# Attention scores in a one-core ViT block: keys spread by DMA replaced by 32-row tiles of TensorE

## The reference, cut to what matters

```python
q1 = heads(x @ Q1_w.T);  k1 = heads(x @ K1_w.T + K1_b)      # heads: 8 of width 16
q2 = heads(x @ Q2_w.T);  k2 = heads(x @ K2_w.T + K2_b)
a1 = softmax(einsum('bhqd,bhkd->bhqk', q1, k1) / scale)
a2 = softmax(einsum('bhqd,bhkd->bhqk', q2, k2) / scale)
attn = a1 - lam * a2
o = einsum('bhqk,bhkd->bhqd', attn, v)
```

## Time and profile before

| | |
|---|---|
| median of 3 runs | 238.61 us |
| lowest and highest run | 237.48 and 258.14 us |
| profiled execution, its own time | 233.28 us |
| its span, first to last instruction | 231.5 us |
| PE busy | 181.9 us (79%) |
| DVE busy | 150.4 us (65%) |
| ACT busy | 102.6 us (44%) |
| POOL busy | 47.6 us (21%) |
| TensorE clock granted, mean | 0.884 |

### The profile page before, as it was taken

The page is one execution under the profiler, slowest core; times in us unless marked ns, Lnnn a source line. Parts: engine busy times, 40 slices in busy tenths (PEclk is TensorE's granted clock), DMA queues, the critical chain, the costliest instruction groups (busy, mean ns, idle before and its releaser), DMA issues.

```text
span 231.5 us, 8246 instructions
## 1 busy us (share of the span) xinstructions
PE 181.9 (79%) x3649; PEld 142.6 (62%) x3649; DVE 150.4 (65%) x335; ACT 102.6 (44%) x185; POOL 47.6 (21%) x64
## 2 busy tenths in 40 slices
PE   0799989999186595787899999999999999992000
PEld 0799975558144364675478888788887787871000
DVE  1333596567459999789965776666555454468960
ACT  2000047557213322413353667776775343325882
POOL 0000007302508668300000000000007000007660
PEclk9999999999859855558999999999999999998555
DMA  6999994253446400000000222131200000000012
GB/s 228 396 391 387 401 146 98 78 129 92 117 107 141 92 6 3 4 3 0 4 0 3 52 58 78 30 96 34 80 5 3 3 6 3 3 3 4 28 45 71
DMA packets 11108, 19.83 MB, mean 86 GB/s; under 512 B 2030, under 2 KB 6830, under 8 KB 10432
## 3 DMA queue, kind: packets, MB, share of 16 engines
q1 hardware_dynamic: 11072, 19.30, 28.5%
HBM read 15.20 MB, written 0.82 MB: 69 GB/s over the span
## 4 chain that ended last, share of the span: by engine, by line
PE 47%; DVE 31%; SPq 6%; issue 5%; ACT 4%; DMA 3%; POOL 2%; ACTq 0%; POOLq 0%
PE PS L1086 14%; PE PS L898 10%; DVE arena L302 7%; PE PS L1108 7%; PE PS L1098 4%; DVE t L649 3%; SPq L363 3%; DVE sm L703 2%; DVE mx L691 2%; ACT t L610 2%; SPq L350 2%; DVE st L851 2%; PE PS L1056 2%; PE PS L935 2%; DMA hid<-conv_filter 2%
## 5 line engine op out<-in xcount | busy, mean ns | idle before, releaser
L302 DVE COPY arena<-PS 128x1024 f32<-128x1024 f32 x32 | 39.0, 1224 | 32.4 <-PE PS L1086 32.4
L301 ACT ACTIVATE arena<-PS 128x1024 f32<-128x1024 f32 x32 | 32.7, 1025 | 22.4 <-PE PS L1086 22.3
L1086 PE MATMUL PS<-gates,wrow 18*128 18x128 f32 x1024 | 37.2, 282 | 1.7 <-DVE arena L302 0.7
L1086 PEld LDWEIGHTS PS<-gates,wrow 18*128 18x128 f32 x1024 | 31.4, 186 | 7.9 <-DVE arena L302 5.0
L898 PE MATMUL PS<-hid,arena 128*128 128x128 f32 (+1 forms) x208 | 26.7, 288 | 7.3 <-DVE hid L628 7.3
L898 PEld LDWEIGHTS PS<-hid,arena 128*128 128x128 f32 (+1 forms) x208 | 25.2, 198 | 8.7 <-issue 8.3
L957 PE MATMUL PS<-hid,arena 128*32 128x200 f32 x256 | 16.7, 421 | 10.0 <-DMA hid<-arena 10.0
L628 DVE TENSOR_REDUCE hid<-hid 128x256 f32<-128x1280 f32 x4 | 9.5, 2369 | 16.8 <-DMA hid<-conv_filter 16.8
L459 ACT ACTIVATE sd<-mv,epsc 128x2 f32<-128x2 f32 (+1 forms) x15 | 4.3, 292 | 35.7 <-DVE mv L639 35.7
L957 PEld LDWEIGHTS PS<-hid,arena 128*32 128x32 f32 x256 | 9.2, 132 | 16.3 <-DMA hid<-arena 11.8
L1108 PE MATMUL PS<-arena,t 128*32 128x128 f32 x512 | 17.3, 276 | 0.0
(11 more groups left out here) (106 smaller groups left out, 294.1 us busy)
## 6 DMA issues: line engine op xcount, KB each, us to landing
arena<-windows SPq DMA_DIRECT2D x24, 256.0 KB, 7.9
wrow<-ffn_weights SPq DMA_DIRECT2D x32, 128.0 KB
hid<-arena SPq DMA_DIRECT2D x32, 100.0 KB, 2.2
hid<-conv_filter SPq DMA_DIRECT2D x4, 640.0 KB, 7.3
cst<-consts SPq DMA_DIRECT2D x1, 1098.0 KB, 16.6
wrow<-ffn_weights SPq DMA_DIRECT2D x64, 8.0 KB
out<-t SPq DMA_DIRECT2D x16, 50.0 KB
arena<-windows SPq DMA_DIRECT2D x4, 64.0 KB, 8.1
```

Source lines behind the costliest of these rows:

```text
L301: return eng.activation(dst, PS[:, b:b + 2, :], ACT.Copy)
L302: return eng.tensor_copy(dst, PS[:, b:b + 2, :])
L1086: mm = pe.matmul(PS[:, merge_bank(n) + r, :].rearrange("p (b k j) -> p k b j", k=4, j=NJ)[:, k], wrow[32 * r:32 * r + KR, w], gates[32 * r ...
```

## The change

The spread keys go, and with them the zeroed buffer, its semaphores and the 32 DMAs. `scores(u)` takes its keys straight from `kX`. It now goes by 32-channel blocks r = 0 to 3: for each block, each b and each of the 8 images one matmul, whose stationary operand is 32 channels by 32 query columns (partitions 32r to 32r+31) and whose moving operand is 32 channels by 50 columns (25 keys with the odd head zeroed, 25 with the even one zeroed). That is 64 matmuls of 50 columns a step, where there were 16 of 200. Blocks 0 and 2 write one PSUM bank, blocks 1 and 3 the other; between block 1 and block 2, PE waits until its own last matmul of block 1 is done (`half_scored`). Each step waits for all four projections of its images instead of the spread keys. The scores of a step lie in another order of heads, so the layouts of `E`, `prob`, `probT` and of the weights `lamw` change with them; the number and size of these operations stays as it was.

```diff
-        prob = take(2 * 4 * H * 32).rearrange("p (n g h k) -> p n g h k", n=2, g=4, h=H)
-        kE = hid[:, 0:2 * 2 * H * UI * NS].rearrange("p (s b h i k) -> p s b h i k", s=2, b=2, h=H, i=UI)
-        kEd = hid[:, 0:2 * 2 * H * UI * NS].rearrange("p (s b r c) -> p s b r c", s=2, b=2, r=4)
+        prob = take(2 * 4 * H * 32).rearrange("p (n r x k) -> p n r x k", n=2, r=4, x=8)
...
-            def spread_keys(u):
-                if u % 2 == 0:
-                    sp.wait_ge(proj_ready[1], 2 * (u // 2 + 1))
-                    sp.wait_ge(proj_ready[3], 2 * (u // 2 + 1))
-                if u < 2:
-                    sp.wait_ge(spread_zeroed, u + 1)
-                else:
-                    sp.wait_ge(scores_done, u - 1)
-                for r in range(4):
-                    f = slice(32 * r, 32 * r + 32)
-                    sp.dma_start(kEd[f, u % 2, :, r, :], kX[f, u].rearrange("p b m k -> p b (m k)")).then_inc(keys_spread[u % 2], 16)
-            for c in range(NC - 1):
+            for c in range(NC):
                 load_rows(0, c)
-            spread_keys(0)
-            spread_keys(1)
-            load_rows(0, NC - 1)
-            for u in range(2, NU8):
-                spread_keys(u)
...
-            for i in range(2):
-                pool.memset(kEd[:, i], 0.0).then_inc(spread_zeroed, 1)
...
-                e4 = E[:, slot, :].rearrange("p (g b h k) -> p g b h k", g=2, b=2, k=NS)
-                pool.tensor_tensor(prob[:, n % 2, g:g + 2, :, 0:NS], e4[:, :, 0], e4[:, :, 1],
-                                   ALU.add).then_inc(prob_done, 1)
+                e4 = E[:, slot, :].rearrange("p (r b x k) -> p r b x k", r=4, b=2, k=NS)
+                pool.tensor_tensor(prob[:, n % 2, :, x:x + 4, 0:NS], e4[:, :, 0], e4[:, :, 1], ALU.add).then_inc(prob_done, 1)
...
             def scores(u):
                 slot = u % 2
-                pe.wait_ge(keys_spread[slot], 16 * 4 * (u // 2 + 1))
+                for w in range(4):
+                    pe.wait_ge(proj_ready[w], (2 if w in (1, 3) else 1) * (u // 2 + 1))
                 if u >= 2:
                     pe.wait_ge(shifted, u - 1)
-                for g in range(2):
+                for r in range(4):
+                    f = slice(32 * r, 32 * r + 32)
+                    if r == 2:
+                        mm.then_inc(half_scored, 1)
+                        pe.wait_ge(half_scored, u + 1)
                     for b in range(2):
-                        for i in range(4):
-                            im = u * UI + g * 4 + i
-                            mm = pe.matmul(PS[32 * i:32 * i + 32, 2 * slot + g, b * H * NS:(b + 1) * H * NS],
-                                           qT[b][:, im * NS:im * NS + 32], kE[:, slot, b, :, g * 4 + i, :], start=True, stop=True)
+                        for il in range(UI):
+                            im = u * UI + il
+                            c = (r // 2) * 8 * NS + b * 4 * NS + (il // 4) * 2 * NS
+                            mm = pe.matmul(PS[32 * (il % 4):32 * (il % 4) + 32, 2 * slot + r % 2, c:c + 2 * NS],
+                                           qT[b][f, im * NS:im * NS + 32], kX[f, u, b, :, il * NS:(il + 1) * NS], start=True, stop=True)
                 mm.then_inc(scores_done, 1)
```

More of the change, by code:

```diff
@@ L139, in build @@
         E = take(ES * UC).rearrange("p (u c) -> p u c", u=ES)
-        prob = take(2 * 4 * H * 32).rearrange("p (n g h k) -> p n g h k", n=2, g=4, h=H)
-        kE = hid[:, 0:2 * 2 * H * UI * NS].rearrange("p (s b h i k) -> p s b h i k", s=2, b=2, h=H, i=UI)
-        kEd = hid[:, 0:2 * 2 * H * UI * NS].rearrange("p (s b r c) -> p s b r c", s=2, b=2, r=4)
-        probT = t6[:, 0:2 * 4 * H * 32].rearrange("p (n g h q) -> p n g h q", n=2, g=4, h=H)
+        prob = take(2 * 4 * H * 32).rearrange("p (n r x k) -> p n r x k", n=2, r=4, x=8)
+        probT = t6[:, 0:2 * 4 * H * 32].rearrange("p (n r x q) -> p n r x q", n=2, r=4, x=8)
         otmp = t5[:, NTOK:NTOK + QT].rearrange("p (i g q) -> p i g q", i=4, g=4)
@@ L205, in build @@
         probs_zeroed = sem("probs_zeroed")
-        spread_zeroed = sem("spread_zeroed")
-        keys_spread = [sem(f"keys_spread{i}") for i in range(2)]
         proj_done = [sem(f"proj_done{w}") for w in range(4)]
@@ L216, in build @@
         hb_ready = sem("hb_ready")
+        half_scored = sem("half_scored")
         scores_done = sem("scores_done")
@@ L401, in _ @@
             pool.memset(t4[:, NTOK:TP], 0.0).then_inc(pads_set, 1)
-            for i in range(2):
-                pool.memset(kEd[:, i], 0.0).then_inc(spread_zeroed, 1)
             pool.wait_ge(neglam_ready, 2)
             pool.wait_ge(eps_set, 3)
-            lv = lamw[:, :].rearrange("p (g b h) -> p g b h", g=2, b=2)
+            lv = lamw[:, :].rearrange("p (r a b g m) -> p r a b g m", r=2, a=2, b=2, g=2)
             for g in range(2):
-                pool.tensor_copy(lv[:, g, 1, :], neglam[:, H:2 * H]).then_inc(lamw_ready, 1)
+                pool.tensor_copy(lv[:, :, :, 1, g], neglam[:, H:2 * H].rearrange("p (a r m) -> p r a m", a=2, r=2)).then_inc(lamw_ready, 1)
             pool.memset(prob[:, :, :, :, :], 0.0).then_inc(probs_zeroed, 1)
@@ L415, in _ @@
             for u in range(NU8):
-                n, g, slot = u // 2, 2 * (u % 2), u % ES
+                n, x, slot = u // 2, 4 * (u % 2), u % ES
                 c = slice(UX * slot, UX * slot + UX)
@@ L713, in prob_transpose @@
                     dve.wait_ge(pv_done, 2 * (n - 1))
-                dve.transpose(probT[:, n % 2].rearrange("p g h q -> p (g h q)"),
-                              prob[:, n % 2].rearrange("p g h k -> p (g h k)")).then_inc(probT_done, 1)
+                dve.transpose(probT[:, n % 2].rearrange("p r x q -> p (r x q)"),
+                              prob[:, n % 2].rearrange("p r x k -> p (r x k)")).then_inc(probT_done, 1)
             oT = t1[:, 0:NTOK].rearrange("p (n g i q) -> p n i g q", n=NQ, g=4, i=4)
@@ L971, in values @@
                                            vtok[32 * i:32 * i + 32, 4 * n + g, 32 * r:32 * r + 32],
-                                           probT[32 * i:32 * i + 32, n % 2, g, 2 * r:2 * r + 2, 0:NS], start=True, stop=True)
+                                           probT[32 * i:32 * i + 32, n % 2, 2 * (r % 2) + r // 2, 2 * g:2 * g + 2, 0:NS], start=True, stop=True)
                 mm.then_inc(pv_done, 1)
```

## The result

The changed kernel's median is 239.4 us over 20 runs, that of the kernel before 237.53 over 20 runs beside it; the ratio is 1.0126, with a 95% interval of 1.0069 to 1.0182. The forecast was 233.2 us, its range ended at 236.7. Executions of either kernel fall into a faster and a slower state, and a ratio with an interval is that of the faster ones alone, while medians and profiles can be of either; the two medians lie only 0.8% apart.

What follows compares the result with a forecast made beforehand. Step 2's spread keys, late behind SP's row DMAs, left DVE a 5.76 us hole; the third maximum 5.4 us earlier and other terms at 0 gave 238.6 - 5.4 = 233.2 us; range 232.4 to 234.1, 8 in 10 230.7 to 236.7.

Steps and rivals of the forecast that it cites:

- What bounds the kernel: Attention stage: step 2's spread keys queue behind SP's 12 row DMAs, leaving DVE a hole of 5.76 us.
- The sum up to the third maximum: PE from scores(0) through v_proj to step 2: DVE's third maximum at about 60.9 instead of 66.27, 5.4 us earlier.
- A quarter of the rows and four times the matmuls come to the same PE time; I take a difference of 0: PE score step at full clock: 1.34 us for 128 new records against 1.37 before, counted as no change.
- PE stays ahead of DVE by 1.5 us or more: Steps 3 to 7: PE finishes scores before DVE asks, so the 5.4 us gain stays.
- The middle wait: PE's wait for its own block 1 before block 2: 0.25 us each, bounds 0 and 0.6, on the path three times.
- the later five lie under DVE and cost nothing: Of eight middle waits, only those in steps 0, 1 and 2 lie on the path; later ones cost 0.
- The rival of the clock: Under 32-row scores TensorE's clock partly falls, costing 1.5 to 3.5 us; gain 2 to 4, 234.7 to 236.7; chance 0.23.
- The rival of a gain taken up later: Middle waits of 0.6 and a slower POOL add cut the gain to 3.4 us, 235.2; chance 0.09.
- POOL's add: L430 in POOL's last steps gets another output loop level: taken as 0, bounds 0 and +0.5 us each.
- The slower rival: Clock lost from step 0 through step 2: third maximum 1.7 us later than before, 240.3 us; chance 0.05.
- The 25 ns of the Trainium skill's page on TensorE: Minimum start-to-start time per matmul: 64 would take 1.6 us, gain 0.8 us less over three steps; set aside.

Runs made afterwards that it cites:

- pairs kernel: Changed kernel with 32 score matmuls of 100 columns a step instead of 64 of 50, half the scores being of wrong images; ratio 0.9768.
- kept up by filling: Changed kernel with two unread 128-row matmuls of 400 columns between scores(0) and scores(1); median 241.62 us against 237.33 for the kernel before.
- 24 waits: Changed kernel with PE waiting for its own last matmul between all four blocks of a step, 24 waits instead of 8; ratio 1.0178.
- rows-last kernel: Kernel before with the weight rows for c = 3 issued behind all key spreads; median 232.35 us against 234.65, again 233.29 against 237.61.
- the filling: rows-last kernel with two 128x128 matmuls ahead of each of merges 1 to 3; median 231.71 us against 237.33, again 232.13 against 237.61.

## Why the prediction was wrong, step by step

**What bounds the kernel** held. SP's 12 row DMAs made step 2 late, and putting them elsewhere alone moved the third maximum from 14.0 to 8.5 us behind the start of scores(0).

**The sum up to the third maximum** held for the work that it counted. Forecast 8.7 us; the pairs kernel, with the same tiles, columns and middle waits and half the instructions, has 8.1. The changed kernel has 13.2. The 4.5 over the forecast are the first stop (1.4), 2.3 for v_proj at the lower clock, and the rest mainly the last 50 records of scores(1) at the lower clock. So up to here more is lost to the clock, which fell in the stop, than to the stop itself.

**"A quarter of the rows and four times the matmuls come to the same PE time; I take a difference of 0"** is the step that failed. It was worked out from bursts of 64 records of L970 with idle time or other work around them. 10.5 ns from start to start is about right within a burst: 206 records took 3.0 us with two middle waits in them, which leaves some 11 ns for each. It is wrong for 1280 records in 35 us, since a block of 127 or so takes 3.4 to 3.8 us to come: 27 to 30 ns for each. A step of 128 records thus took 3.4 us or more where 1.34 at the full clock and 2.46 at half had been counted. No row of before could show this price, as no stretch there asked for a second block so soon; but its counts did say how many records a step had before and would have after, and I had turned them into array time alone. The bounds of this term should have reached to a price for each instruction.

**"PE stays ahead of DVE by 1.5 us or more"** fell with it. With stops, steps 3 to 6 were just in time or 0.2 us late, and step 7, with two values(k) of 64 records among the steps ahead of it, 2.0 late. From the third to the eighth maximum it took 21.6 us instead of 19.3.

**The middle wait** was well sized, 0.25 us forecast and 0.25 measured; the 0.05 in it for a hand-over came from no row, so the last hundredths are luck. That the later five lie under DVE and cost nothing was wrong, once PE was the late one: by the scaling above, some 0.1 to 0.2 us each.

**The rival of the clock** was given 0.23 for 2 to 4 us of gain left, and its sight was half right: the clock did fall ahead of v_proj. But under the same tiles without a stop it stayed up to 63.7 us (pairs), and where it was kept up by filling, the time didn't fall. **The rival of a gain taken up later** named POOL's add and the middle waits; the add went on as before and POOL was never what DVE waited for. **The slower rival** had its loss from the clock alone, 1.7 us; the measured loss has nearly this size for another reason, and the agreement is chance. Its sum also took 2.74 us for v_proj, which is the time of two score steps; v_proj takes 3.5 (58.45 - 54.98, both in its own sum). With that the path is 7.5 us and not 6.8, and the rival's time 241.0.

**The 25 ns of the Trainium skill's page on TensorE** ("TensorE: Matmul & The Clock Gate", Part 1) were weighed against the rows and set aside. The rows within a burst still speak against them: 21 ns a matmul, or 10.5 if each record is counted as one. The limit measured over a long stretch, 54 to 60 ns for a matmul of two records, is in neither.

## What to carry to other kernels

Count the instructions as well as the columns: on PE, a float32 matmul is two records here, each with a weight load, and over a long stretch 128 records came no faster than one block in some 3.5 us. A measured rate from a short burst holds for that burst; before multiplying it, ask whether any stretch of the trace kept it up for as long as the change will. And before replacing a transfer that comes late, look at what stands ahead of it in its queue: moving three lines of SP's program closed the hole that the new score path was built to close.

## What the runs showed of the hardware

The times of the packets look like a loop with a nearly steady delay: a 16 KB packet, PE's restart 2.2 to 2.7 us behind it, the next packet 1.0 to 1.7 us behind the restart. Slower work on PE thus isn't fully absorbed by the stops: with 24 waits the stops lost some 0.5 us each, and the time from restart to restart grew by some 0.5. The stops appear in the trace only as idle time that is put down to nothing ("issue"), at fixed counts of records.

The clock can stay at half while PE is busy the whole time: it did from 126 to 134 us in the rows-last kernel (8.00 of 8.00 us). It had fallen behind 18-row merges with PE busy 4.04 of 4.50 us. Profiles with this half clock have 150.4 to 150.7 us behind the eighth maximum (149.3 in one where it was shorter), those without it 146.0 to 146.1 (147.5 with the filling), so it costs up to 4.7 us, nearly as much as the whole change was expected to bring.
